# An attention and expert layer on one core: another order of the attention loop, a norm on ScalarE, a product on GpSimd, paired slot weights and a second table in eight steps

## What is computed

```python
h = _layernorm(x) * (1 + ca) + sa
q, k = _rope(h @ Wq), _rope(h @ Wk); v = h @ Wv          # 4 heads of 32
sk = clip(h @ sk_w1 @ sk_w2 + sk_b2, -32, 32)            # 4 heads x 64 slots
sv = clip(h @ sv_w1 @ sv_w2 + sv_b2, -32, 32)
wk, wv = exp(sk), exp(sv);  zk, zv = cumsum(wk), cumsum(wv)
S = where(mask, q k^T, 0)
p = softmax(S wk * scale / zk)
A = where(mask, (p / zv) wv^T, 0)
o = A v
on = o * rsqrt(mean(o * o) + EPS) * gnorm_w
x = x + ga * ((on * g * sigmoid(g)) @ Wo)                # g = h @ Wg
h = _layernorm(x) * (1 + cb) + sb                        # then a norm, a router, top 2 of 8
eo = gelu(xn @ w1[e] + b1[e]) @ w2[e] + b2[e]
x = x + gb * (layernorm(weighted sum of the two) * out_ln_w + out_ln_b)
```

## Time and profile before

| | us |
|---|---|
| median of 3 runs | 498.81 (498.32 to 500.5) |
| the profiled execution's own time | 499.39 |
| its span, first to last instruction | 497.6 |

### The profile page before, as it was taken

The page is one execution under the profiler, slowest core; times in us unless marked ns, Lnnn a source line. Parts: engine busy times, 40 slices in busy tenths (PEclk is TensorE's granted clock), DMA queues, the critical chain, the costliest instruction groups (busy, mean ns, idle before and its releaser), DMA issues.

```text
span 497.6 us, 11499 instructions
## 1 busy us (share of the span) xinstructions
PE 436.6 (88%) x3266; PEld 363.0 (73%) x3266; DVE 398.8 (80%) x1134; ACT 316.9 (64%) x813; POOL 347.0 (70%) x404
## 2 busy tenths in 40 slices
PE   3589999999899899899899766699889999999990
PEld 1366777776677677677677544599889999999980
DVE  2579999999989989989989975467677677786385
ACT  1166778888578678678688645565545555555574
POOL 4675865689979989989987546267567656665632
PEclk9999999999889889889999958599999999999996
DMA  6950000000000000000000050235434322226344
GB/s 152 236 160 0 7 8 5 2 18 19 25 17 19 23 19 19 24 17 19 24 22 14 18 193 23 54 75 175 148 91 105 90 72 69 73 65 229 118 137 125
DMA packets 33934, 33.66 MB, mean 68 GB/s; under 512 B 7037, under 2 KB 27681, under 8 KB 33745
## 3 DMA queue, kind: packets, MB, share of 16 engines
q1 hardware_dynamic: 27600, 22.39, 16.7%
q0 software_dynamic: 4320, 9.22, 5.5%
q10 hardware_dynamic: 1952, 1.32, 1.1%
HBM read 20.43 MB, written 12.48 MB: 66 GB/s over the span
## 4 chain that ended last, share of the span: by engine, by line
PE 49%; POOL 23%; DVE 16%; issue 6%; ACT 4%; DVEq 1%; DMA 0%; ACTq 0%; POOLq 0%
PE sa_ps L1625 12%; POOL xe_dram L388 8%; PE sa_ps L1635 6%; PE bank L1635 6%; PE sa_ps L1403 3%; POOL lgs L422 3%; POOL A_sb L395 3%; PE bank L1616 2%; POOL xn L473 2%; PE bank L1475 2%; POOL kT L445 2%; PE sa_ps L1396 2%; PE bank L1476 2%; PE bank L1600 2%; PE bank L1542 2%
## 5 line engine op out<-in xcount | busy, mean ns | idle before, releaser
L738 ACT ACTIVATE work<-sa_ps,work 128x128 f32<-128x128 f32 x284 | 81.0, 368 | 63.8 <-PE sa_ps L1625 61.9
L483 POOL DMA_INDIRECT y_dram<-work,idxr x71 | 72.4, 1020 | 44.8 <-DVE idxr L1203 32.4
L388 POOL DMA_INDIRECT xe_dram<-xrow,slot x64 | 72.6, 1134 | 24.5 <-issue 14.0
L1625 PE MATMUL sa_ps<-work 128*128 128x128 f32 x568 | 79.4, 284 | 0.0
L1625 PEld LDWEIGHTS sa_ps<-work 128*128 128x128 f32 x568 | 70.5, 195 | 0.2 <-DVE work L1210 0.2
L1403 PE MATMUL sa_ps<-Px,wvT 64*128 64x128 f32 (+1 forms) x288 | 41.4, 338 | 3.8 <-DVE Px L1106 3.7
L1403 PEld LDWEIGHTS sa_ps<-Px,wvT 64*128 64x128 f32 x288 | 33.7, 192 | 13.8 <-DVE Px L1106 9.2
L422 POOL TENSOR_TENSOR lgs<-lgs,rsum 128x256 f32<-128x256 f32 x32 | 30.6, 973 | 18.6 <-DVE rsum L1066 18.6
L1635 PE MATMUL bank<-w2s,work 128*128 x280 | 37.3, 276 | 2.7 <-DVE work L1245 2.7
L1635 PE MATMUL sa_ps<-w2s,work 128*128 x288 | 38.6, 278 | 0.9 <-DVE work L1245 0.6
L395 POOL TENSOR_SCALAR_AFFINE_SELECT A_sb<-A_sb 128x768 f32<-128x768 f32 (+1 forms) x32 | 19.9, 645 | 25.9 <-ACT A_sb L706 25.8
(11 more groups left out here) (280 smaller groups left out, 1119.8 us busy)
## 6 DMA issues: line engine op xcount, KB each, us to landing
work<-xe_dram SPq DMA_DIRECT2D x71, 69.5 KB
work<-in_w SPq DMA_DIRECT2D x1, 2048.0 KB, 9.8
outf<-outf_dram SPq DMA_DIRECT2D x1, 2048.0 KB, 9.8
xrow<-y_dram SPq DMA_DIRECT2D x4, 512.0 KB, 7.4
out<-x_sb SPq DMA_DIRECT2D x7, 256.0 KB, 2.6
y_dram<-work,idxr POOLq DMA_INDIRECT x71, 2.4
modb<-mod_dram SPq DMA_DIRECT2D x16, 64.0 KB, 2.8
xe_dram<-xrow,slot POOLq DMA_INDIRECT x64
```

The costliest lines, as they stand in the source:

```text
L388: nc.gpsimd.indirect_dma_start(xe_dram, bass.IndirectOffsetOnAxis(slot[:, 4 * batch + column:4 * batch + column + 1], 0), xrow[:, tile, :] ...
L483: nc.gpsimd.indirect_dma_start(y_dram, bass.IndirectOffsetOnAxis(idxr[:, n % RING["scat"]:n % RING["scat"] + 1], 0), y[:, n % RING["scat"] ...
L738: last = nc.scalar.activation(hid[:, n % 2, c, :], up_bank[n % 2][:, c * P:(c + 1) * P], ACT.Gelu, bias=w1c[:, n % 3, FF + c:FF + c + 1])
L1625: last = mm(up_bank[n % 2][:, c * P:(c + 1) * P], w1c[:, n % 3, c * P:(c + 1) * P], xgT[:, n % 3, :], start=True, stop=True)
```

## The change

1. The second table is made in eight steps, `late_step`, in `prepare` of tiles 14, 16, ... 28. The second pair of routing gates moves from tiles 20 and 26 to 21 and 27.
2. The first norm: `xn` is made by ScalarE from `rs1` and a new column `nm1` = -mean times `rs1`, which GpSimd makes in two instructions.
3. The product with the gate, the second `onT`, moves from VectorE to GpSimd.
4. `low1` spreads the low-rank columns so that `lT` has 128 rows, in four groups of 32 (16 values, a row of ones for the bias). `low2` holds the four parts of the slot weights in these groups. Parts 0 and 2 are multiplied first, 1 and 3 after the transposition of `xn`.
5. The order of the loop, now 22 iterations. Stages: moments of the first norm 1 (before 0), `hT` and q, k 2 (3), `wkT` transposed, v, clips, sums, 1/z, first clip of g 3 (4), gate 4 (5), difference, exponential, `psum`, `rsum` 4 (5), A mask and `oT` 6 (5), second norm 7 (6), choose 8 (7), place 9 (8), scatters 10 (9).
6. What is left behind the loop is less: no piece of batch 15 before its second norm. The scatters of batches 12 to 15 are strung among fewer tiles.
7. The loads of the expert outputs 1 to 5 share one semaphore.

The new orders of one iteration, with stages in brackets:

- TensorE: lT and g (3), oT (6), fourth head's scores (4), pT (5), slot weights 0, 2 (3), xT (2), slot weights 1, 3 (3), head norm (6), A (5), xn2T (7), lg (4), v (3), A rest (5), h3 (7), lg transposed (4), q and k (2), output (6), wkT transposed (3), scores (3), rank (8).
- VectorE: moments (1), place (9), sums of the second norm (7), rotation (3), choose (8), sums of the first (0), moments of the second (7), Px (5), z times r0 (4), xn2 (7), clip of g (3), t1 (6), rz (4), clips (3), lg2 (4), sums of wv (3), maximum, difference (4), sums of wk (3), x1 (6), psum, rsum (4).
- ScalarE: lT, g (3), square (6), S copy (4), rs2 (7), hT (2), rs (6), exp wk (3), h2T (7), exp wv (3), sigmoid (4), v copy (3), xn (1), A copy (5), h3 and its square (7), exp (4), rs3 (7), wk copy (3), xrow (7), 1/z (3).
- GpSimd: A mask (6), Wob (6), pnorm (5), scatter (10), ve, rs, nm1 (1), scatter (10), S mask (4), qT, kT (3), two scatters (10), gate product (6), gate (4).

```diff
-TAIL = 21
+TAIL = 22
...
-        low1 = sb("low1", [P, 2 * LOW])
-        low2 = sb("low2", [P, 4, P])
+        low1 = sb("low1", [P, P])
+        one_rows = sb("one_rows", [P, 1])[:]
+        low2 = sb("low2", [P, P])
...
-        LOADS = ((0,), (1, 2), (3, 4, 5), (6, 7))
+        LOADS = ((0,), (1, 2, 3, 4, 5), (6, 7))
...
+        LATE_STEPS = range(14, 30, 2)
...
-            sp.dma_start(low1[:, 0:LOW], inp["sk_w1"]).then_inc(S["ld_w"], 16)
-            sp.dma_start(low1[:, LOW:2 * LOW], inp["sv_w1"]).then_inc(S["ld_w"], 16)
+            sp.wait_ge(S["set_zero"], 1)
+            for n in range(4):
+                sp.dma_start(low1[:, 32 * n + 1:32 * n + 1 + LOW], inp["sk_w1" if n < 2 else "sv_w1"]).then_inc(S["ld_w"], 16)
...
-                    nc.gpsimd.tensor_tensor(rs1[:, b % 4], ve1[:], halves[:], ALU.pow).then_inc(S["rstd1_rdy"], 1)
+                    nc.gpsimd.tensor_tensor(rs1[:, b % 4], ve1[:], halves[:], ALU.pow).then_inc(S["root1_rdy"], 1)
+                    need_apart(pool, "root1_rdy", b)
+                    for tile in range(2):
+                        last = nc.gpsimd.tensor_scalar(nm1[:, b % 4, tile:tile + 1], mv1[:, b % 4, tile, 0:1], rs1[:, b % 4, tile:tile + 1], -1.0, ALU.mult, ALU.mult)
+                    last.then_inc(S["rstd1_rdy"], 1)
...
-                    need_apart(pool, "rstd1_rdy", b)
-                    for tile in range(2):
-                        last = nc.gpsimd.tensor_scalar(xn[:, b % 2, tile, :], x_sb[:, 2 * b + tile, :], mv1[:, b % 4, tile, 0:1], rs1[:, b % 4, tile:tile + 1],
-                                                       ALU.subtract, ALU.mult)
-                    last.then_inc(S["xn_rdy"], 1)
...
+                b = i - 6
+                if live(b):
+                    need(pool, "t1_rdy", b)
+                    need(pool, "gate_rdy", b)
+                    nc.gpsimd.tensor_tensor(onT[:, b % 2, :], onT1[:], gate[:, b % 4, :], ALU.mult).then_inc(S["on_rdy"], 1)
...
+            for n in range(4):
+                w2, bias, part = ("sk_w2", "sv_w2")[n // 2], ("sk_b2", "sv_b2")[n // 2], slice(n % 2 * P, (n % 2 + 1) * P)
+                act.dma_start(low2[32 * n + 1:32 * n + 1 + LOW, :], inp[w2][:, part]).then_inc(S["low2_ld"], 16)
+                act.dma_start(low2[32 * n:32 * n + 1, :], inp[bias][part].unsqueeze(0)).then_inc(S["low2_ld"], 16)
...
+                    nc.scalar.activation(lT[:, b % 2, :], b3[:, T:2 * T], ACT.Identity, bias=one_rows).then_inc(S["lT_rdy"], 1)
...
+                b = i - 1
+                if live(b):
+                    need(act, "rstd1_rdy", b)
+                    for tile in range(2):
+                        last = nc.scalar.activation(xn[:, b % 2, tile, :], x_sb[:, 2 * b + tile, :], ACT.Identity, scale=rs1[:, b % 4, tile:tile + 1],
+                                                    bias=nm1[:, b % 4, tile:tile + 1])
+                    last.then_inc(S["xn_rdy"], 1)
...
-                if n == 14:
-                    late_counts()
-                if n == 15:
-                    late_bins()
-                if n == 16:
-                    tile_bins(NS - NA, 2 * NE)
-                if n == 17:
-                    late_experts()
-                if n == 18:
-                    tile_rows(NS - NA, 2 * NE)
-                if n == 19:
-                    late_rows()
...
+                if n in LATE_STEPS:
+                    dve.wait_ge(S["dve_chain"], chain[0])
+                    late_step(LATE_STEPS.index(n))
...
+            def late_step(k):
+
+                n, v = NS - NA, 2 * NE
+                pv = past[:, 0:v * n].rearrange("p (e s) -> p e s", e=v)
+                by_tile = pv.rearrange("p e s -> p s e")
...
+                if k == 2:
+                    mark(nc.vector.tensor_tensor(pv, iota_j[:, 0:n].unsqueeze(1).broadcast_to([1, v, n]), tend[:, 0:v].unsqueeze(2).broadcast_to([1, v, n]), ALU.is_ge))
+                if k == 3:
+                    mark(nc.vector.tensor_reduce(exp_f[:, 0:n], by_tile, AX.X, ALU.add))
+                if k == 4:
+                    link(nc.vector.scalar_tensor_tensor(out=exp_f[:, 0:n], in0=past[:, (NE - 1) * n:NE * n], scalar=-float(NE), in1=exp_f[:, 0:n], op0=ALU.mult, op1=ALU.add))
+                    mark(nc.vector.tensor_scalar(exp_i[:, NA:NS], exp_f[:, 0:n], float(NE - 1), None, ALU.min))
+                if k == 5:
+                    mark(nc.vector.tensor_tensor(pv, pv, jump[:, 0:v].unsqueeze(2).broadcast_to([1, v, n]), ALU.mult))
+                if k == 6:
+                    mark(nc.vector.tensor_reduce(row_f[:, 0:n], by_tile, AX.X, ALU.add))
+                if k == 7:
+                    link(nc.vector.scalar_tensor_tensor(out=row_f[:, 0:n], in0=row_f[:, 0:n], scalar=first[:, 0:1], in1=iota_j[:, 0:n], op0=ALU.add, op1=ALU.add))
+                    nc.vector.tensor_scalar(row_i[:, NA:NS], row_f[:, 0:n], float(P), None, ALU.mult).then_inc(S["table_rdy"], 1)
 
...
+                b = i - 3
+                if live(b):
+                    if b == 0:
+                        pe.wait_ge(S["low2_ld"], 128)
+                    need(pe, "lT_rdy", b)
+                    need(pe, "ropemul_rdy", b)
+                    for n in (0, 2):
+                        rows = slice(32 * n, 32 * n + 32)
+                        last = mm((b4, b5)[n // 2][:, (n % 2) * T:(n % 2 + 1) * T], low2[rows, :], lT[rows, b % 2, :], start=True, stop=True)
+                    last.then_inc(S["skv_mm"], 1)
...
+                b = i - 3
+                if live(b):
+                    need(pe, "skv_mm", b)
+                    for n in (1, 3):
+                        rows = slice(32 * n, 32 * n + 32)
+                        last = mm((b4, b5)[n // 2][:, (n % 2) * T:(n % 2 + 1) * T], low2[rows, :], lT[rows, b % 2, :], start=True, stop=True)
+                    last.then_inc(S["skv2_mm"], 1)
...
-                    for n in range(4):
-                        last = mm((b4, b5)[n // 2][:, (n % 2) * T:(n % 2 + 1) * T], low2[:, n, :], lT[:, b % 2, :], start=True, stop=True)
-                    last.then_inc(S["skv_mm"], 1)
...
+                    need(pe, "sq_rdy", b)
+                    need(pe, "px_rdy", b + 1)
+                    mm(b6[:, 0:T], headmean[:], sq[:], start=True, stop=True).then_inc(S["ms_mm"], 1)
```

753 lines of the change are left out of this document (320 added, 433 removed).

## The result

The changed kernel took 507.69 us (median of 4 runs, 506.15 to 508.13), the kernel before 499.65 beside it (4 runs, 498.32 to 501.73). The ratio is 1.0138, with a 95% interval of 1.0110 to 1.0167. The forecast was 489.9 us in a range of 480 to 498, so size and sign were wrong. The profiled execution has a span of 506.4 us, against 497.6.

A forecast was written before the change was run, and what follows sets the result against it. No engine was full over a pair of iterations; a chain hopping between engines bound the long one, with GpSimd's 17.6 us taken after. Terms 5.0 - 1.1 - 6.7 - 1.1 - 1.0 - 4.0 = -8.9 gave 489.9 us, range 480 to 498.

The forecast's parts named there:

- The fill and the light iterations: Start of the attention loop: first score products at 29.0 us, filling +5.0 us; iterations 7 and 8 from 15.7 to 15.1.
- a net 0.6 in the sum: Row-tiled slot weights on TensorE: 0.6 us gained in the first regime, nothing in the second.
- The second regime: Nine attention iterations with scatters, from 114.0 us on: 156.0 us for 162.7, a gain of 6.7 us.
- GpSimd's own 17.6: Scatter iterations of the attention loop: GpSimd's work taken as the bound, seven iterations at 17.6 us each.
- rival A: Attention loop: the loop over GpSimd's gate product binds, 19.6 us per iteration, 508 us in total; chance 0.12.
- The drain: After the last score products: first gather at +37 us, first up-projection at +42 for +43.1, a gain of 1.1 us.
- the last `Px` at +22: Drain: the last Px comes 22 us after the last score products, with place and table ahead of it; before, 30 us.
- a credit of 1.0 in the first tiles: Tiles 0 to 16: 1.0 us given back of 2.5, as batch 15's output, norm and routing lie among them.
- The second table: Tile loop: steps on every second tile instead of consecutive ones gain 4.0 us, between 0 and 4.3.
- B: Attention loop: nothing comes of the order, pairs of iterations stay near 36.5 us, 495.2 us in total; chance 0.21.
- C: Attention loop: 16.9 us per iteration, near VectorE's busy time, clock at 1.00, filling 2 us cheaper, 482.2 us; chance 0.19.
- The sign named last: Disproof: a pair of 37 or more with GpSimd waiting for `rsum`, or TensorE waiting for ScalarE at the new norm.

The follow-up runs named there:

- e4: Changed kernel with two drain moves: first table behind the last Px, batch 11's four scatters ahead of iteration 21's mask; 506.72 us, ratio 1.0126.
- e7: Kernel before with only the first norm's scaling moved from GpSimd to ScalarE, plus two small GpSimd products; 507.60 us, ratio 1.0104.
- e12: Kernel before with the eight-step second table and three filler products where TensorE waits for the mask of A; 489.16 us, ratio 0.9721.
- e6: Changed kernel with the gate product back on VectorE; 503.80 us, ratio 1.0026 to the kernel before.
- e14: Changed kernel with filler products ahead of the head mean and two extra 128x256 GpSimd products in iterations with the choice; 504.92 us, single execution.
- e11: Changed kernel with second norm's scaling on ScalarE, two filler products ahead of the head mean, and the kernel before's drain order; 493.88 us, ratio 0.9891.
- e3: Changed kernel with two filler products on TensorE ahead of its wait for Px, in iterations with the choice; 504.71 us, ratio 1.0078.
- e10: Changed kernel with the last stretch ordered as before on four engines, table behind last Px, two batch 11 scatters earlier; 500.39 us, ratio 1.0008.
- e1: Kernel before with only the second table of tiles made in eight steps; 497.95 us, ratio 0.9949.
- e13: Changed kernel with ScalarE second-norm scaling, filler products and old drain order, plus the gate product back on VectorE; 503.24 us, ratio 1.0024.
- e8: Changed kernel with first tile's steps inside iteration 21, first table behind last Px, two batch 11 scatters earlier; 509.29 us, ratio 1.0148.

## Why the prediction was wrong, point by point

**The fill and the light iterations** were right in their start and their pace: first score products at 29.0 us as forecast (27.8 to 30.8 in the other runs with this order), the light iteration at 15.3 for 15.1. The slot weights take (11.7 + 11.2) / 16 = 1.43 us per batch by TensorE's groups by line, 0.56 less than the earlier trace rows, for a net 0.6 in the sum. ScalarE's two activations for the norm take 0.88 us for the 0.58 taken. But the clock falls once during the fill (33.9 to 40.7 us) and once in iteration 9 (109.0 to 115.8), where before it stayed up; these two iterations are 2.0 and 2.4 us longer than before, and the sum had priced all filling at the clock of the rows. Iteration 9 is 18.9 us here and 16.9 in e4, the same program up to there with the clock at 1.00, so 2.0 of its 2.4 us are the low clock of this execution.

**The second regime** failed at the step "so GpSimd's own 17.6 is taken". An iteration took 18.8 us (half of 37.6), with GpSimd busy 15.1 of it. Two things were wrong in the step. First, I summed busy times of GpSimd and took the largest sum for the bound, though I had written that no engine is full over a pair. GpSimd's busy time in a pair was to be 33.2 and measured 30.2, and it has 2% of the chain. e7 takes 3.75 us from GpSimd's 33.38 in a pair of the kernel before, and TensorE's later `hT` uses up what that frees. What set a pair of the kernel before was a path over several engines, with TensorE's products at half clock in it (e12: 2.0 and 0.6 us of 37.0 come back with the clock alone). I had read the 0.84 of the earlier trace rows as a result of idling, not as a price. Second, I counted VectorE's operations at their lengths of before: 33.0 per pair. It measures 34.5. Beside GpSimd's new order other operations of VectorE are the long ones: over all batches `rz` takes 27.9 us for 23.1, `xn2` 18.7 for 11.2, `z` 23.4 for 20.7, 15.0 more together by VectorE's groups by line, while the eight scans of the choice take 2.5 for 8.2. The balance is 1.5 us a pair over the 33.0, more than the gate product had cost (0.85 a pair), and what grew stands in the chain. How the 1.5 us divides between the order and the product on GpSimd is not shown: with the product back on VectorE `rz` takes 21.6 us, but `xn2` and the scans of `wvT` stay long or grow (e6).

Of the holds the prediction spoke in rival A, and took their victim for GpSimd: its sums and scatters would grow and close a loop of 19.6 us. GpSimd's work in the pair fell instead, from 33.4 to 30.2, and VectorE paid. A's number, 508, was met by the measurement (nine times its 19.6 against my 156.0 would make it 510), but that is luck, as its mechanism isn't the one: e6 takes the loop through GpSimd's product away and its pairs are at 37.1 and 38.0. The Trainium skill (SBUF — State Buffer, SBUF: two separate sides) says that whichever engine starts first has the shared ports for a whole instruction and the other blocks. `xn2`, 2.63 us for 0.60 and ending with GpSimd's `kT`, agrees, and so does e14. I had applied the rule mainly in one direction.

**The drain** failed at "I get the first up-projection at +42"; it is +51.4. Three steps of it were off. The last `rsum` was to come early enough for the last `Px` at +22, and that `Px` came at +29.4 (+20.8 in e11), with the clock at 0.5 from +4.9 us on: the last `rsum` is at +22.9 here, at +19.4 in e3, +17.3 in e6 and +16.5 in e11, where the clock is up for longer in the first 20 us of the drain. Then, the steps of iteration 21 that precede the first tile on TensorE and ScalarE (second norm of batch 14, output and residual of batch 15, the second norm of batch 15 before the first GELU) were counted as done beside it. They take 12.1 us from the start of the last `oT` products to the first up product, for 6.9 before, and another 4.5 to the first GELU, for 2.1. e10 puts the order of before back and gains 4.9 us by the GELU of tile 10. I had given that work a credit of 1.0 in the first tiles. Last, the early table and the late gather, on which my working spent most of its words, decided next to nothing (e4).

**The second table** was right: -4.0 forecast, -3.9 in the tile loop of e1, -4.4 where it stood. The whole tile loop gave 4.7 for the 5.0 forecast.

**The rivals.** B (pairs near 36.5) and C (near VectorE's busy time, clock at 1.00) both took it that the clock would be no worse than before. None of the cases had the clock as the mechanism, though the earlier trace rows had it at 0.70 in the drain, and none had a longer drain or longer operations of VectorE in its time. The range ended at 498, 9.7 us below the result. The sign named last came half true: a pair of over 37 us, with GpSimd standing 0.98 us for `rsum`.

What stays open: why the tile loop of e10, e6 and e13 runs 117 us from the GELU of tile 10 to that of the last tile and that of the others with the new table 119 to 120 (evenly, 1.94 to 1.95 us per tile for 1.98 to 2.00), and what decides whether the clock falls at a wait. Row-tiled slot weights weren't tried alone, nor the clock held up through the drain by filler products. In e11 one long iteration of the middle is still 20.95 us.

## What to carry to other kernels

Where no engine is full, relieving the busiest one need not give anything: follow the chain, and look for a second one of the same length before pricing the first. A short wait of TensorE can cost more by the clock behind it than by itself; a few products with unused results in front of the wait are a quick test, and gave 2.3% here by the ratios of e12 and e1, where some 900 changed lines lost 1.4%. In the changed order the same filler gave 0.6%. If work of a last batch is put ahead of the next stage, go through every engine's queue for what now stands behind it.

## What the runs showed of the hardware

- In the kernel before, a wait of TensorE of 1.59 us is followed by 6.8 us at a granted clock of 0.5, once in a pair (3.4 in the last); with 0.29 us left of it the clock stays at 1.00 through two pairs (e12), in one of them in spite of another wait of 1.72 us. In the changed kernel the fall comes 0.5 us ahead of a wait of 1.29 us.
- Executions of one and the same loop differ in their low stretches: 10.2 us per pair in the changed kernel, 6.8 in e4, e8 and e10, with pairs of 37.3 to 37.8 us in all four.
- VectorE's operations with all operands in SBUF grow beside GpSimd's: two of 128x128 from 0.60 to 2.63 us, one of 128x1024 from 1.21 to 2.99, a pair of scans from 1.26 to 2.58. Those that read PSUM (`Px`, `lg`, `mx`) stay at 0.65 to 0.69 in every iteration of every run.
- A 128x1 product with two column operands on GpSimd takes 0.26 us at the median (0.50 for the two) and 0.46 on average, as some take up to 1.31; 0.40 was estimated.
- The scaling of the first norm takes ScalarE 0.88 us per batch, and took GpSimd 1.97 (31.5 / 16).
